# Waits of neighbouring score bursts gathered ahead of the first burst on TensorE

## The reference

```python
q = axial_rope(layernorm(x) @ Wq);  k, v = split(ctx @ Wkv);  k = axial_rope(k)
logits = einsum('bqhd,bkhd->bhqk', q, k) / sqrt(8)
x = x + einsum('bhqk,bkhd->bqhd', softmax(logits), v).reshape(b, n, 256) @ Wout + bout
h = layernorm(x)
shared = square(relu(h @ up_w)) @ down_w                      # 256 -> 1024 -> 256
moe = (h @ expert_weight) * top_2(h @ gate_w).sum(-1)
x = x + layernorm(shared + moe) * gamma + beta
```

## The kernel before

| bursts | item ahead | a bank of the last burst | item behind |
|---|---|---|---|
| B.0.3, B.0.4, B.0.5 | xT.1.0 | of xT.1.0, emptied by ScalarE | B.0.6 |
| B.6, B.7 | PV.1 | of PV.1, emptied by ScalarE | MT.5 |
| B.10, B.11 | PV.3 | of PV.3, emptied by ScalarE | o.0 |
| B.12, B.13 | PV.4 | of MT.7, emptied by ScalarE | MT.8 |
| B.14, B.15 | PV.5 | of ST 6.1 (`ex`); B.15 also waits for `sM.7` | W.0 |
| B.17, B.18 | PV.6 | of S 11.1, emptied by VectorE (`rd`) | PV.7 |
| B.39, B.40 | dnb.0 | of dn.0, emptied by VectorE | PV.18 |
| B.61, B.62, B.63, B.64 | up0.2 | of up0.2, emptied by ScalarE (L660) | up0.3 |

## Time and profile before

### The profile page before, as it was taken

One profiled execution on the slowest core, in us unless ns is written; L12 is line 12 of the kernel. 1 busy time (PEld: TensorE's weight loads), 2 busy tenths in 40 slices (PEclk: granted clock), 3 DMA queues, 4 the chain that ended last, 5 costly groups with the idle time before them and its releaser, 6 DMA issues.

```text
span 209.0 us, 6609 instructions
## 1 busy us (share of the span) xinstructions
PE 190.0 (91%) x2506; PEld 161.0 (77%) x2506; DVE 142.8 (68%) x297; ACT 120.5 (58%) x275; POOL 84.5 (40%) x169
## 2 busy tenths in 40 slices
PE   3989498878899999999999999999999999999990
PEld 2889376656777878888777888778999988999980
DVE  1689497998899888678899986775420558245324
ACT  5743433579788987858676777769572111421400
POOL 6549787982933202410472314121211116263203
PEclk9999958999999999999999999999999999999997
DMA  6919632486544300000042000000000000000001
GB/s 165 313 30 271 130 85 47 107 241 181 168 129 106 108 9 6 3 3 3 5 125 62 5 3 8 5 3 28 5 3 0 28 22 31 0 2 3 25 0 50
DMA packets 15999, 13.15 MB, mean 63 GB/s; under 512 B 2912, under 2 KB 15584, under 8 KB 15968
## 3 DMA queue, kind: packets, MB, share of 16 engines
q1 hardware_dynamic: 11136, 9.32, 15.9%
q10 hardware_dynamic: 4832, 3.42, 6.4%
HBM read 5.13 MB, written 1.05 MB: 30 GB/s over the span
## 4 chain that ended last, share of the span: by engine, by line
PE 66%; DMA 10%; SPq 6%; DVE 4%; issue 4%; POOL 3%; ACT 3%; ACTq 1%; POOLq 0%; DVEq 0%
PE ps L823 24%; PE ps L991 12%; PE ps L940 10%; PE ps L856 9%; PE ps L817 6%; PE ps L846 4%; DMA qstack<-mT 3%; SPq L377 3%; DMA x_sb<-in_x 3%; DMA qstack<-hi_q 2%; ACT probs L627 2%; DMA kstack<-lo_k 1%; SPq L437 1%; ACTq L377 1%; DVE xn L409 1%
## 5 line engine op out<-in xcount | busy, mean ns | idle before, releaser
L744 DVE TENSOR_REDUCE mneg<-ps 128x2 f32<-128x512 f32 x128 | 81.0, 683 | 15.2 <-PE ps L846 15.0
L627 ACT ACTIVATE probs<-ps 128x512 f32<-128x512 f32 x128 | 69.1, 595 | 15.3 <-PE ps L856 13.9
L856 PEld LDWEIGHTS ps<-qstack,kstack 32*128 32x128 f32 x512 | 32.7, 185 | 14.6 <-issue 10.3
L856 PE MATMUL ps<-qstack,kstack 32*128 32x128 f32 x512 | 40.0, 282 | 3.2 <-DMA qstack<-mT 1.5
L940 PE MATMUL ps<-probs,vaug 128*32 128x128 f32 x1024 | 34.0, 275 | 0.6 <-ACT probs L627 0.4
L846 PE MATMUL ps<-kstack,qstack 32*128 32x256 f32 x256 | 32.0, 338 | 2.5 <-DMA qstack<-hi_q 2.1
L823 PE MATMUL ps<-x2nT,up 128*128 128x128 f32 x256 | 31.0, 276 | 0.1
L823 PEld LDWEIGHTS ps<-x2nT,up 128*128 128x128 f32 x256 | 30.2, 192 | 0.7 <-issue 0.2
L991 PE MATMUL ps<-down,inner 128*128 128x256 f32 x128 | 29.5, 379 | 0.0
L940 PEld LDWEIGHTS ps<-probs,vaug 128*32 128x32 f32 x1024 | 26.3, 109 | 3.5 <-issue 1.6
L536 POOL TENSOR_SCALAR mnat<-mneg 128x8 fp32r<-128x8 f32 x32 | 7.6, 236 | 49.2 <-DVE mneg L744 37.8
(11 more groups left out here) (95 smaller groups left out, 251.9 us busy)
## 6 DMA issues: line engine op xcount, KB each, us to landing
kstack<-hi_k SPq DMA_DIRECT2D x12, 128.0 KB, 2.6
qstack<-hi_q SPq DMA_DIRECT2D x11, 128.0 KB, 3.1
kstack<-lo_k SPq DMA_DIRECT2D x8, 128.0 KB, 2.5
result<-x_sb SPq DMA_DIRECT2D x8, 128.0 KB, 1.7
down<-in_L_ffn_down_w ACTq DMA_DIRECT2D x3, 256.0 KB, 4.1
qstack<-lo_q SPq DMA_DIRECT2D x5, 128.0 KB, 2.6
x_sb<-in_x SPq DMA_DIRECT2D x2, 256.0 KB, 5.1
up<-in_L_ffn_up_w SPq DMA_DIRECT2D x1, 512.0 KB, 6.6
```

The lines of the kernel that those rows point to most:

```text
L627: act.activation(probs[M % NPROBS][:, i, :, :, :], bg(("ST", M, i))[:].rearrange("p (s t n) -> p s t n", s=2, t=T), ACT.Exp, scale=SCALE). ...
L744: emptied(dve.tensor_reduce(mneg[M % NNEG][:, i, :], bg(("S", M, i))[:].rearrange("p (s k) -> p s k", s=2), AX.X, ALU.max, negate=True), ( ...
L856: return pe.matmul(bg(("ST", M, i))[:, at:at + P], kstack[b % 2][strip(i), 2 * m + s, tile(k)], qstack[b][strip(i), 2 * m + s, tile(t)], s ...
```

## The change

Bursts that follow each other in `PE_ORDER` form a run, as long as no burst needs a bank that an earlier burst of the same run fills. Ahead of the first burst of a run TensorE now waits for the former holders of the banks of all its bursts (again one wait for each emptying engine, the last) and for the transfers that any of its bursts needs. Ahead of the other bursts of the run it waits for nothing. For a burst that stands alone, the wait for the stacked keys and queries moves from the first `S` product to the head of the burst. The orders, banks, products and all other engines' programs are as before.

By this rule 31 bursts stand alone, 16 runs have two bursts, two have three (B.0.3 to B.0.5; B.57 to B.59) and one has four (B.61 to B.64): 23 bursts are not the first of their run.

```diff
+    RUN, run, seen = {}, [], set()
+    for e in pe_order:
+        units = units_of(e)
+        needs = {BEFORE[u] for u in units} | ({LAST_EX[e[1]]} if e[0] == "PV" else set())
+        if e[0] not in ("B",) or run and needs & seen:
+            run, seen = [], set()
+        if e[0] in ("B",):
+            run.append(e)
+            seen.update(units)
+            RUN[e] = run
...
-            def banks_of_burst(units):
+            def banks_of_run(units):
...
+            def wait_for_run(e):
+
+                if RUN[e][0] != e:
+                    return
+                banks_of_run([u for each in RUN[e] for u in units_of(each)])
+                for each in RUN[e]:
+                    what = each[0]
+                    for kind, *unit in burst_units(each) if what == "B" else []:
+                        if kind == "ST":
+                            transposed_wait(*unit)
+                        else:
+                            plain_wait(*unit)
...
                 if what == "B":
                     units = burst_units(e)
-                    banks_of_burst(units)
+                    wait_for_run(e)
                     for s in range(2):
                         for k in range(2):
                             for kind, M, i in units:
                                 if kind == "ST":
-                                    if s == 0 and k == 0:
-                                        transposed_wait(M, i)
                                     ins = transposed(M, i, s, k)
...
                                 elif k == 0:
-                                    if s == 0:
-                                        plain_wait(M, i)
                                     ins = plain(M, i, s)
```

## The result

The changed kernel takes 221.22 us (median of 4 runs, 220.19 to 222.38), the kernel before 212.26 (4 runs beside it, 209.63 to 213.84). The ratio of the times is 1.047, with a 95% interval of 1.034 to 1.059. (Some executions of a kernel come out over 1.5% slower than its fastest; medians here are of all executions, ratios leave those out.) The profiled execution took 220.43 us, 9.66 more than the one of before (210.77); its span is 218.6 us. 220.1 was forecast.

What follows compares the result with a forecast made beforehand. The prediction took TensorE to set the pace, in the long windows especially. Gathered runs at 8.6 us plus early runs at 0.7 made 9.3 us, added to the profiled 210.8 for 220.1 us; range 215.0 to 223.5.

Steps and rivals of the forecast that it cites:

- The sum: Whole kernel: 8.6 us for the gathered runs plus 0.7 for the early ones, 9.3 us slower; this forecast got 0.60.
- the run's offset: At each run: time from the first burst's first weight load to the last burst's, 0.49 to 1.06 us, predicted as its price.
- The step that failed: At B.12 and B.13: their 0.63 us delay would vanish because B.14 waits for B.15's transfer until 61.80 us anyway.
- What is late next: At B.39 and B.40: PV.18 late by some 0.8 us, B.41's transfer of keys eating 0.6; 0.3 counted of 1.06.
- The early part: Ahead of B.9: early runs cost 0.7 us (bounds 0.2 and 1.2), B.6 and B.7 some 0.3 of their 0.60.
- The windows: Stretches 62 to 101 and 111 to 150 us: same work takes 3 to 4 us more each, TensorE's busy time nearly unchanged.
- Only TensorE's time: Rival, all runs: ScalarE and VectorE catch up, so a run of two costs 0.45 us; 6.3 in all, 217.1 us; chance 0.20.
- Hidden: Rival, all runs: ScalarE's backlog of earlier exponentials covers the late first burst; no cost, 210.8 or 208.5 us; chance 0.12.
- The saved waits: At the 23 bursts not first in a run: up to 46 waits of 0.051 us, 2.3 us at most; taken as 0.
- The clock falls: Rival: new idle times bring one more 6.8 us stretch at largely 1.2 GHz, costing 3.4 us more, 223.5 us; chance 0.08.

## Why the prediction was right

**The sum.** 9.3 us forecast, 9.66 measured, and for the reason given: the first burst comes late by the run's offset, and everything behind by nearly the same. From B.10 on it is 8.3 forecast and 8.3 measured. Nine of the fourteen prices from B.10 on are within 0.1 us of the forecast.

**The step that failed** is B.12 and B.13: "The delay of 0.63 ends before that: nothing is left." I had counted on B.14's new wait for a transfer at 61.80 us, a time read in the trace of before, where the end of that exponential of ST 6.1 lay just as late (61.60). But that exponential works on B.13's own scores: when the run is late, so is it. The transfer doesn't move with the run, since it brings maxima that TensorE transposes ahead of B.12. SyncE issues it 1.6 us later than before, no more than PV.4, ahead of B.12, is late already (1.62); with the 2.47 us that it took before it would land at about 63.3, an estimate. In the timelines of the kernels before and after:

```profile
59.20 0.63 SPq L465 DMA_DIRECT2D qstack<-mT  x1
```

```profile
60.80 0.63 SPq L476 DMA_DIRECT2D qstack<-mT  x1
```

The chain that holds B.14, in the timeline of the kernel after:

```profile
59.69 0.43 DVE L765 TENSOR_TENSOR attn<-ps,rden 128x256 f32<-128x256 f32 x1
...
60.17 0.33 PE L867 MATMUL ps<-qstack,kstack 32*128 32x128 f32 x2 [0.70 <-DVE attn L765]
...
60.86 0.60 ACT L638 ACTIVATE probs<-ps 128x512 f32<-128x512 f32 x1 [0.91 <-PE ps L867]
...
63.40 0.59 ACT L638 ACTIVATE probs<-ps 128x512 f32<-128x512 f32 x1
64.09 0.33 PE L867 MATMUL ps<-qstack,kstack 32*128 32x128 f32 x2 [0.92 <-ACT probs L638]
```

B.12 waits for VectorE, 60.17; ST 6.1's exponential ends at 63.99, 2.4 us later than before; B.14 starts behind it at 64.09. So the bank is what holds B.14. The price was 0.78, not 0, and the run by itself cost 0.96. The step failed because the prediction looked only at which wait ends last in the old trace, and not at what feeds the other one. That the sum still fits is luck: B.10, B.14, B.17, B.29, B.45 and B.57 were each 0.07 to 0.21 too dear in the forecast, probably because the products of a run, packed behind its wait, make up a little of the late start; no run isolates that.

**What is late next** was right at B.39: PV.18 late by some 0.8 (0.79 measured), of which B.41's transfer ate most (0.28 left). It was right, too, that nothing is lost behind 151 us of the old time.

**The early part** was forecast at 1.0 up to B.9 and came out at 1.34. No run shows that the early runs cost this: 0.36 of it is there at B.0.1 already, and executions that gather nothing ahead of B.9 come to PV.3 0.49 us earlier to 2.47 later than before.

**The windows** should have grown by 3 to 4 us each: 2.65 and 3.6. The prediction's own offsets gave only 2.6 for the four runs in the first; I wrote the same span for both without adding. Nor did TensorE's busy time stay nearly the same: it fell by 1.2 us in each, by the packing.

**The rivals.** *Only TensorE's time*, 0.45 us a run, is refuted by B.26 (0.71), B.29 (0.76), B.42 (0.68) and B.14 (0.87). At B.29 the timeline of the kernel after shows the engines starved in full:

```profile
91.56 0.33 PE L867 MATMUL ps<-qstack,kstack 32*128 32x128 f32 x2 [0.72 <-ACT mT L567]
...
92.19 1.29 DVE L755 TENSOR_REDUCE mneg<-ps 128x2 f32<-128x512 f32 x2 [2.36 <-PE ps L857]
...
92.29 1.57 ACT L638 ACTIVATE probs<-ps 128x512 f32<-128x512 f32 x3 [0.78 <-PE ps L867]
...
93.03 0.41 PE L828 MATMUL ps<-ident,c_sb 128*128 128x128 f32 x2 [0.52 <-ACT probs L638]
```

TensorE is idle ahead of the run, VectorE and ScalarE until it delivers, and TensorE again until ScalarE has emptied a bank. *Hidden* needed a backlog on ScalarE. From B.10 on no run came free; all cost over half of their offset but B.39, whose delay a transfer ate. The saved waits, 2.3 us at the very most, were worth 0.2 or less. B.61 to B.64 show the packing at its best, in the timeline of the kernel after:

```profile
158.18 0.60 ACT L671 ACTIVATE whole<-ps 128x512 f32<-128x512 f32 x1 [0.87 <-PE ps L834]
...
158.83 1.03 PEld L867 LDWEIGHTS ps<-qstack,kstack 32*128 32x128 f32 x32 [0.94 <-ACT whole L671]
158.83 1.17 PE L867 MATMUL ps<-qstack,kstack 32*128 32x128 f32 x32 [0.75 <-ACT whole L671]
159.52 1.08 ACT L638 ACTIVATE probs<-ps 128x512 f32<-128x512 f32 x2 [0.75 <-PE ps L867]
```

Thirty-two products in 1.17 us, and still 0.81 us lost, because all four bursts wait for ScalarE's pass at 158.18 that only the last needs. The Trainium skill (Perfetto Trace Analysis, Matmul Optimizations) wants matmuls back to back in batches. Here the traces show no gain by it: the batches are tighter, the granted clock was 1.00 with and without them in the long windows, and the batch's price was the wait for its last bank.

*The clock falls* did not come in the changed kernel's profile. It did come in experiments, at the price that the rival had named (below).

## What to carry to other kernels

A wait put at the head of a batch costs the distance from the head to the last thing in it, here nearly in full, if the engines behind are starved until the batch delivers; ask first whether they have a backlog. Gather only what is free by then (that cost 0.2 us at most here, but saves nothing that can be seen either: the satisfied waits hid behind the products). And when a delay seems to end at some later wait, see what ends that wait: where it is the delayed work's own output, it moves along.

## What had not been expected

The granted clock fell to 0.50 (1.2 GHz) in single executions, for 3.4 to 13.6 us, in the middle of the kernel, and not always with the same kernel. The kernel before isn't free of it either: of its 17 executions beside the last experiments the longest took 224.77 us, at a mean granted clock of 0.90 (0.97 to 0.98 in the shortest ones). The one with only B.12 and B.13 gathered had it at 53.7 to 67.4 us in one execution and, beyond its early stretch, not at all there in the other. In three of the kernels it fell within 1.4 us of the start of B.60. Windows of the kernel with only the later runs gathered, and of the one with all waits kept:

```profile
140.00:144.80 4.80, 3.19 (x82) 2.66 (x82) 4.15 (x9) 3.03 (x7) 1.23 (x4) 1.00 0.02 6
144.80:151.60 6.80, 6.80 (x53) 5.51 (x54) 0.82 (x4) 3.88 (x10) 0.13 (x1) 0.50 0.06 20
```

```profile
148.90:153.70 4.80, 3.52 (x93) 3.10 (x96) 3.27 (x6) 4.05 (x10) 1.14 (x3) 1.00 0.10 32
...
153.70:157.10 3.40, 3.40 (x23) 2.31 (x14) 0.34 (x2) 2.23 (x6) 0.00 (x0) 0.50 0.00 0
```

Ahead of the fall TensorE was busy for 3.19 of 4.80 us and 3.52 of 4.80, never idle for more than 0.49 us at a time; during it, without a pause. The two stretches cost 3.2 and 1.6 us, near half their length each; the prediction's rival had priced 6.8 us at 3.4. The changed kernel has the same gathered runs at this place and kept 1.00 in its profile, so idle time of this size doesn't settle it. What does stays open. For this kernel it means that a single time can be off by more than the price of five runs, and that executions are to be read item by item, with the clock beside them.
